# Two pairs of transposes and one group of down products, moved within the feed-forward of batch 0 of a decoder layer

## The reference, cut to what matters

```
x = layernorm(x + attention(x))                       # 16 heads of 128, quantized weights
Q = x @ W_q.T                                         # cross attention, one head of 512
s = coef * (Q @ ctx.T);  s -= max(s)                  # (2, 512, 1024)
s = where(s < 54th largest of its row, -inf, s)
x = layernorm(x + (softmax(s) @ ctx) @ W_o.T)
gate, up = split(x @ W_gate_up.T)                     # 2048 columns each
x = layernorm(x + (silu(gate) * up) @ W_down.T)
```

## Time and profile before

| | |
|---|---|
| time, median of 3 runs | 944.97 us (943.44 to 947.11) |
| profiled execution, its time | 945.73 us |
| profiled execution, its span | 943.9 us, 13220 instructions |
| PE busy | 912.9 us, 97% of the span |
| DVE, ACT, POOL busy | 593.0, 575.5, 491.8 us |
| HBM, mean over the span | 81 GB/s |

### The profile page before, as it was taken

How to read it: one execution, slowest core, us unless ns; L and a number is a source line. 1 busy time by engine, 2 the same in 40 slices (tenths; PEclk the granted TensorE clock), 3 DMA queues, 4 the chain that set the end, 5 groups by cost and what they waited for, 6 DMA issues and landing times.

```text
span 943.9 us, 13220 instructions
## 1 busy us (share of the span) xinstructions
PE 912.9 (97%) x4440; PEld 750.1 (79%) x4440; DVE 593.0 (63%) x1066; ACT 575.5 (61%) x1142; POOL 491.8 (52%) x407
## 2 busy tenths in 40 slices
PE   8999999999999999999989889899999899999997
PEld 7788788887888877887868678798878788888885
DVE  5666966669666686658694899975878125411114
ACT  4667876678766787778874366533755534443333
POOL 4357752556526466477743467534764741354440
PEclk9999999999999999999999999899999999999999
DMA  7531230212302223123112303323433331343321
GB/s 202 157 104 53 86 89 1 61 58 75 100 1 54 64 74 84 46 72 86 54 43 83 90 23 101 104 76 100 124 91 99 104 112 41 112 122 94 94 83 44
DMA packets 46102, 76.97 MB, mean 82 GB/s; under 512 B 5584, under 2 KB 11216, under 8 KB 45776
## 3 DMA queue, kind: packets, MB, share of 16 engines
q1 hardware_dynamic: 45600, 75.68, 27.2%
q10 hardware_dynamic: 432, 0.39, 0.2%
HBM read 73.69 MB, written 2.36 MB: 81 GB/s over the span
## 4 chain that ended last, share of the span: by engine, by line
PE 40%; DVE 8%; ACT 2%; issue 2%; POOL 1%; ACTq 0%; DVEq 0%; POOLq 0%
PE p L895 6%; PE p L896 6%; PE p L899 6%; PE p L909 3%; PE p L910 3%; PE p L911 3%; DVE m L1561 1%; PE p L861 1%; PE p L862 1%; PE p L863 1%; PE p L776 1%; PE p L774 1%; PE p L773 1%; DVE acc L1522 1%; DVE st L1529 1%
## 5 line engine op out<-in xcount | busy, mean ns | idle before, releaser
L1983 POOL TENSOR_TENSOR V<-RAW,V 128x512 fp32r<-128x512 f32 x64 | 82.4, 1309 | 142.1 <-ACT V L1078 142.1
L1496 DVE TENSOR_SCALAR_CACHE_REDUCE JK<-p,ssc 128x512 bf16<-128x512 f32 x112 | 83.7, 747 | 112.9 <-PE p L660 112.9
L1024 ACT ACTIVATE PR<-p,nms,ssc 128x512 f32<-128x512 f32 x112 | 87.5, 781 | 60.0 <-DVE JK L1496 58.7
L2068 POOL TENSOR_TENSOR acc<-SX,acc 128x512 f32<-128x512 f32 x54 | 69.8, 1293 | 75.0 <-ACT SX L1058 51.8
L678 PE MATMUL p<-R 128*128 128x512 f32 x248 | 97.3, 392 | 0.8 <-DVE V L1489 0.8
L1983 POOL TENSOR_TENSOR C<-RAW,C 128x512 fp32r<-128x512 f32 x58 | 76.1, 1325 | 41.2 <-ACT C L1078 41.2
L1813 DVE TENSOR_TENSOR SX<-p,SX 128x512 f32<-128x512 f32 x32 | 22.1, 691 | 116.0 <-PE p L899 109.9
L1509 DVE TENSOR_TENSOR PT<-p,PT 128x512 fp32r<-128x512 f32 x128 | 87.4, 683 | 5.4 <-ACT PT L1043 5.2
L713 PEld LDWEIGHTS p<-ident,PR 128*128 128x128 f32 x512 | 62.4, 140 | 21.2 <-DVE PT L1509 6.6
L713 PE MATMUL p<-ident,PR 128*128 128x128 f32 x512 | 77.4, 274 | 1.0
L1043 ACT ACTIVATE PT<-p 128x512 fp32r<-128x512 f32 x128 | 75.8, 592 | 0.7 <-PE p L713 0.7
(11 more groups left out here) (243 smaller groups left out, 2735.9 us busy)
## 6 DMA issues: line engine op xcount, KB each, us to landing
RAW<-in_wg SPq DMA_DIRECT2D x32, 256.0 KB, 2.9
RAW<-in_wu SPq DMA_DIRECT2D x32, 256.0 KB, 2.7
RAW<-in_ctxn SPq DMA_DIRECT2D x32, 256.0 KB, 2.8
RAW<-in_wd SPq DMA_DIRECT2D x32, 256.0 KB, 2.8
RAW<-in_wq SPq DMA_DIRECT2D x19, 256.0 KB, 2.7
RAW<-in_wk SPq DMA_DIRECT2D x18, 256.0 KB, 2.7
RAW<-in_wv SPq DMA_DIRECT2D x16, 256.0 KB, 2.8
RAW<-in_wo SPq DMA_DIRECT2D x16, 256.0 KB, 4.7
```

The costliest lines, as they stand in the source:

```text
L1024: e.activation(PR[:, i % 2, :], P[i % 2][:, :], ACT.Exp, bias=nms[:, i % 4:i % 4 + 1], scale=ssc[:, 0:1] if HB[j][0] > 1 else SC, accum_ou ...
L1496: e.tensor_scalar(JK[:, :], P[i % 2][:, :], ssc[:, 1:2] if HB[i // 4][0] > 1 else -SC, None, ALU.mult, ALU.min, accum_out=nms[:, i % 4:i % ...
L1983: e.tensor_tensor(lo, RAW[:, slot[key], :], hi, ALU.subtract).then_inc(*c_lo.up(key))
L2068: e.tensor_tensor(acc[:, r], OBUF[:, (4 * q + tt) % 2], acc[:, r], ALU.add).then_inc(*rows[r].up((q, 1)))
```

## The change

In block 7 the transposes of the sixth mask tile go from ahead of `gate_up(7)` to behind it. In block 12 those of the eighth go from ahead of `gate_up(12)` to behind it, and then come the down products of block 11, which stood behind the eight value products. ACT's program is changed in the same places: the Silu and high half of blocks 7 and 12 (`gate_act`) go ahead of the copies of the two mask tiles (`px_pair`). The exponentials of the search stay ahead of `gate_act`, as before. A semaphore that nothing used is gone. The programs of DVE, POOL and SP are the same.

```diff
@@ tensor @@
             for n in range(2, 2 * NM + 1):
-                if n == 7:
-                    for hf in range(2):
-                        px_T(5, hf, 6 + hf)
-                if n == 12:
-                    for hf in range(2):
-                        px_T(7, hf, 6 + hf)
...
                 if n < 2 * NM:
                     gate_up(n, (4, 5) if n % 2 or 6 <= n < NM else (6, 7))
-                if n in (6, 11):
+                if n in (6, 7, 11, 12):
                     for hf in range(2):
-                        px_T(4 if n == 6 else 6, hf, 6 + hf)
+                        px_T({6: 4, 7: 5, 11: 6, 12: 7}[n], hf, 6 + hf)
+                if n == 12:
+                    for tt in range(4):
+                        down(n - 1, tt)
                 if n in (12, 13):
...
-                if n < 2 * NM - 2:
+                if n < 2 * NM - 2 and n != 12:
                     for tt in range(4):
                         down(n - 1, tt)
@@ scalar @@
             for n in range(2, 2 * NM + 1):
                 if n in (7, 12):
-                    px_pair(5 if n == 7 else 7)
+                    search(topk.until(5 if n == 7 else 7))
...
                 if n < 2 * NM:
                     gate_act(n, (4, 5) if n % 2 or 6 <= n < NM else (6, 7))
+                if n in (7, 12):
+                    px_pair(5 if n == 7 else 7)
+                if n < 2 * NM:
                     conv_gu(n + 2)
```

More of the change, by code:

```diff
@@ L435, in decoder_layer @@
         gup, silu, gate, h_hi, h_lo, downp = (sig(n) for n in ("gup", "silu", "gate", "h_hi", "h_lo", "downp"))
-        last_bias, last_sum = sig("last_bias"), sig("last_sum")
+        last_bias = sig("last_bias")
         def w_lo(piece):
```

## The result

The changed kernel takes 941.45 us (median of 7 runs, 940.84 to 943.68), the kernel before 946.42 us (7 runs, 943.44 to 949.64). The ratio is 0.9952, with a 95% interval from 0.9933 to 0.9970. I had said 939.9 us in a range from 938.0 to 942.8, a gain of 5.1 us from 944.97. The measured gain is 946.42 - 941.45 = 4.97 us.

What follows compares the result with a forecast made beforehand. PE, busy 97% of the span, was taken to bound the kernel. The terms 1.01 + 4.43 - 0.35 = 5.1 us, taken from the median of 944.97, gave 939.9 us, range 938.0 to 942.8.

Steps and rivals of the forecast that it cites:

- Block 7, 1.01 us: PE, sixth mask tile's transposes behind gate and up: 7.46 us becomes 6.45 us, a gain of 1.01 us.
- Block 12, 4.43 us less a new wait: PE, eighth mask tile's transposes and block 11's down products: 13.60 us becomes 9.17 us, less 0.35 us of new wait.
- The new wait, 0.35 us: PE ahead of block 12's first value product, waiting for POOL's low half: 0.24 us plus 0.10 us for late Silu, rounded.
- T: The end of gate and up of block 12 on PE, forecast at 735.80 us.
- The upper bound of 1.7 us: Largest new wait ahead of block 12's value products, if ACT's handover to POOL took another 1.36 us.
- Covers: Masks, copies, context tiles and banks stay ready in time; the first new context tile's margin grows from 0.8 to 1.8 us.
- Rival A: Block 12's low clock is absent from most executions: 1.6 us less to win, gain 3.5, time 941.5 us; chance 0.17.
- Rival B: PE waits 1.7 us instead of 0.35 ahead of block 12's value products: gain 3.7, time 941.3 us; chance 0.13.
- C: Block 12's new wait vanishes and the median's executions had slower stretches: gain 5.4 to 6, about 939.2 us; chance 0.12.
- E: Transposes would wait for the mask behind gate and up too, needing it 1.8 us later; chance counted within Rival B.
- The larger form of B: The clock also falls behind the wait at block 12's value products, another 1.6 us: gain 2.1, time 942.9 us.
- Rival D: Late context tiles starve value products of blocks 12 and 13 at low clock: 4.5 us slower, 949.5 us; chance 0.03.

Runs made afterwards that it cites:

- the filled kernel: The kernel before, with ten added matmuls in PE's 2.6 us wait ahead of block 12's transposes, their result overwritten; 944.55 us, ratio 0.9990 to before.
- the kernel with one more switch: The changed kernel with one more switch of ACT's function table ahead of block 12's Silu; 943.69 us, ratio 0.9977 to before.
- block 7 alone: The kernel before with only the sixth mask tile's transposes and copies moved, the eighth's left as before; 945.13 us, ratio 0.9996 to before.

## Why the prediction was right, point by point

1. **Block 7, 1.01 us.** Measured from multiply to multiply of blocks 6 and 8: before 703.32 - 684.05 = 19.27 us, after 18.11, so 1.16 us, and 1.22 us in the stretch when made alone. The 0.15 us more are the transposes, which I had put at 1.01 us. I had worked out the free slot ahead of them as 727.60 from DVE's multiply, but the earlier trace rows has them start at 727.70, so they took 728.84 - 0.23 - 727.70 = 0.91 us there, and in the change 694.96 - 0.23 - 693.86 = 0.87 us, in block 12 as well (737.69 - 0.23 - 736.59). The last 0.06 us of the part made alone lie in block 12.
2. **Block 12, 4.43 us less a new wait.** From block 8 to block 14 the gain is 4.95 - 1.16 = 3.79 us, alone 3.79 us. Predicted were 4.43 - 0.35 = 4.08. I also misread: not twelve matmuls of 512 columns start in its 3.51 us but eight, so the low clock takes 3.51 - 8 x 0.2267 = 1.70 us there, which agrees with the 1.64 us of the filled kernel. The gain of 4.43 us itself was read from start to start and holds it.
3. **The new wait, 0.35 us.** This is the term that was mis-sized: 0.50 us idle, and 0.66 us between the free slot (739.97 + 0.23) and the first value product. The 0.3 us missing in block 12 come from here: 0.31 us more of wait and about 0.1 us of slower starts right behind it (740.86 to 741.17 is 0.31 us), less the 0.14 us that the transposes took less. The chain of waits of the kernel after shows its legs:

```profile
734.92 1.28 ACT L1323
736.21 0.01 issue
736.22 0.61 ACT SX L1323
...
736.92 0.70 DVE SX L1813
...
737.64 0.02 ACT C L1330
...
738.66 0.60 ACT R L1306
739.25 0.07 issue
739.32 1.29 POOL R L2034
740.62 0.25 issue
740.86 0.47 PE p L861
```

From T = 736.59 the multiply came at T + 0.33 (I had T + 0.30, with Silu 0.10 us late), POOL's low half started at T + 2.73 (T + 2.70) and was done at T + 4.02. The last leg is what I had wrong: from POOL's end to PE's start there are 0.25 us, and 0.24 or 0.25 us again in the other kernels with this wait. The 0.04 us that I had set came from no row, and the earlier trace rows already showed 0.15 us from DVE's mask to PE (733.98 to 734.13). Why this handover takes 0.25 us stays open. The other 0.1 us is PE itself, which had its slot free at T + 3.61 and not at T + 3.73, by the shorter transposes. The upper bound of 1.7 us rested on a misread row too: the 1.36 us at 733.71 in the earlier trace rows is how long POOL stood idle, not how long ACT's handover took. That Silu and not PE sets the multiply was right: DVE's row above names ACT's L1323, and the kernel with one more switch moves the wait one for one.
4. **Covers.** All held in the change. The first new context tile was ready at 745.61, 2.15 us ahead of its use, where I had 1.8. The margin is real but small: with only the copies ahead of Silu, PE came 0.66 us earlier and POOL's weight tiles 1.5 us later, and it was used up.
5. **Rival A, no low clock in most executions.** Not settled. The clock is low behind the 2.6 us wait in both profiled kernels that have this wait unfilled (before and block 7 alone). But behind the same wait of 1.93 us it fell in seven profiled executions and not in five, and the runs of the kernel with one more switch spread from 942.31 to 945.16 us. If the clock fell before the change in every run, the medians should differ by 4.95 us, and if it never did by 4.95 - 1.64 = 3.31 us. They differ by 4.97 us in the first comparison and by 4.17 us in the later one, which fits both all and a part of the runs. And the time measured, 941.45 us, is also the 941.5 us of this rival: the forecast had the gain, not the time.
6. **Rival B, the wait moves; C, it vanishes; E, the transposes wait for the mask as well.** The wait of the forecast came, at 0.50 us idle where B has 1.7 us and C none. The larger form of B is what the kernels with the down products left behind and with one more switch are, and the version with copies and weight tiles ahead gives C's gain, 102.32 - 96.62 = 5.7 us. For E, the transposes have no idle time ahead of them.
7. **Rival D, starved value products.** Not in the change. Its mechanism exists: it took 0.7 us from the version with the copies ahead, and 1.7 us where the earlier waits were filled. It was never near the 4.5 us slower that I had priced, since in these kernels PE stood only until the late tile was there, and the clock stayed at full behind it.
8. **The sum.** 5.1 predicted, 4.95 in the stretch, 4.97 and 4.17 in the medians. The first value product came 58.20 us behind block 6's multiply before and 55.86 us after, 2.3 us earlier where I had 2.4. The absolute time was forecast 1.5 us too low, for the most part because the median of before is 946.42 over seven runs where three had shown 944.97. Both lie at the edges: the other three sets of before, 15 to 23 runs each, have 945.27 to 945.87. So it is luck in part that the first two medians give the forecast gain within 0.2 us; the stretch, and the two parts made alone, carry it.

## What to carry to other kernels

A step that waits for a slow engine should stand behind work that is ready, and the step that needs its result behind more such work; count the whole chain between the two, queue by queue, and compare it with the cover. A wait of PE of 2 us or more could cost 1.6 us beyond its own length here, where the clock fell behind it, so cover that is missing by 2 us can cost nearly twice that. When an engine in the chain is reordered to shorten it, look at what stood behind the step that now comes later: here it was weight tiles whose buffers the next transfers wanted.

## What the runs showed of the hardware

In the profiled executions the granted clock fell from 2.4 to 1.2 GHz behind waits of PE of 2.0, 2.6, 2.9 and 3.2 us, and behind one of 1.93 us in seven of twelve; it did not fall behind waits of 0.3 to 1.3 us, nor behind the one of 1.7 us. After the fall the matmuls of 512 columns start 0.43 us apart instead of 0.23 us. That lasted some 3.5 us behind the waits of 1.93, 2.0, 2.6 and 3.2 us, and some 7 us behind the one of 2.9 us, which another of 1.2 us follows (0.77 on average over the 15 us from 600). Work without a use in the wait, 10 matmuls of 512 columns or 24 and 12 of 256, kept it up. A switch of ACT's table took 1.28 us and nothing beside it. The handover from POOL's low half of the mask tile to the first value product took 0.25 us, but from POOL's low half of a context tile to the matmul that stood for it 0.06 us (746.29 to 746.35, with the copies ahead). DVE's mask reached PE in 0.15 us before the change (733.98 to 734.13); in the chain above Silu reached DVE in 0.09 us (736.83 to 736.92), the multiply reached ACT in 0.02 us (737.62 to 737.64), and ACT's copy reached POOL in 0.07 us (739.25 to 739.32).
